# Another table of places for the steps of a four-layer transformer block: other order on every engine, other banks

## The chip, the cores and the metric

The kernel runs on one core of one Trainium2 chip. The metric is the device time in microseconds (us) of one execution. TensorE is written PE, VectorE DVE, ScalarE ACT, GpSimd POOL; PEld is the weight load of PE.

## What is computed

Eight samples of 512 rows by 256 columns pass four layers, each added to its input after a layer norm: causal attention with rotary embedding, gated attention over the 256 rows with the largest gate, attention with a relative bias, and gated attention again.

```python
x = x + attn_a(_layernorm(x), Wq, Wk, Wv, Wo)          # 16 heads of 16, rope, causal
x = x + ffn(_layernorm(x), Wg, Wq, Wk, Wv, Wo)         # top 256 of 512 rows by gate, 16 heads of 16
x = x + attn_b(_layernorm(x), w_qkv, w_out, rel_bias)  # 16 heads of 64, scores + bias
x = x + ffn(_layernorm(x), Wg, Wq, Wk, Wv, Wo)
```

Everything is in float32 but a few masks.

## The kernel before

The work is cut into 2264 steps, `Step(kind, s, l, n, q)`: kind, sample s, layer l, and indices n and q. A letter ahead of the kind names the layer: `c_` causal, `f_` gated (l is 1 or 3), `b_` biased. Most steps have a part on PE that fills one, two or four of the eight PSUM banks, and a part on DVE or ACT that empties them (`UNITS` says how many and by whom).

The steps that matter here:

- `b_k`, `b_q`, `b_v`: projections for a pair of heads (line 824), `b_row`: two score products of 64 rows (L1507), then on DVE bias and row maximum (L1229), then the exponential on ACT (L1038); `b_nrm`: reciprocal on DVE (L1238) and scaling on POOL (L961); `b_tr`: eight transposes (L1515), copied by ACT (L1047); `b_val`: the product with the values, in four parts q (L1525); `b_y`: output product (L1271).
- `c_xt`, `b_xt`: transposes of the normed input (L1290), copied by ACT (L980); `c_qk`: the first product that reads the copy of `c_xt` (L824). `c_p1`, `c_m`, `c_p2`, `c_val`: scores with 32 rows for the maxima (L1322, reduced by DVE, L1138), the maxima turned (L1335), scores again with the maxima in them (L1345, exponential on ACT, L998), values (L1359). `c_p1` and `c_p2` take four banks each.
- `f_row`, `f_rank`, `f_spread`, `f_gather`: the gate turned into a row, ranks, and the choice of 256 rows. `f_p1`, `f_m`, `f_p2`, `f_val`: as in the causal layer, for four groups n (L1432 with DVE L1209; L1441; L1450 with ACT L1016; L1462). `f_t1`: the results turned (L1470), divided on DVE (L1158); `f_ot`: turned back (L1478); then `f_o` and `f_y`.

PE runs in four shapes: the full 128 by 128, 32-row tiles (`c_p1`, `c_p2`, `f_p1`, `f_p2`), 64-row tiles (`b_row`), and 32 or 64 columns (`c_val` and `f_val`; `b_val`). The table `TILES` holds them. `c_p1` begins in 32-row tiles and ends in the full array.

What sets the order: `PLACE` gives every step a number. `turn` adds the sample's multiple of `CYCLE`. `in_order` takes, again and again, the step with the lowest number among those whose needs and forerunners are out; only the order comes from the numbers. It hands banks to the steps by its own table of costs (`WORK`). Every engine then walks this one list in order: PE, ACT, DVE, POOL and the queue of SP each issue their part of a step when the list comes to it. An engine that waits for one step holds back all its later ones. Line 842 is where PE's waits are issued (`at_least`).

Rows of the table: `first0`, `first1` and `first` for the causal and gated layers of samples 0 and 1 and the biased layer of sample 0; `cycle` for the causal and first gated layers of samples 2 to 7 and the biased layers of samples 1 to 6; `cycle3` for the last gated layers of samples 0 to 5; `last2`, `last` and `last1` for what ends the run. In the cycle of sample s, from `b_xt` of s to `b_xt` of s + 1, PE works on the biased layer of s, the last gated layer of s - 1, and the causal and first gated layers of s + 1. There are six such cycles with the same order, s = 1 to 6. Each has 240 PE steps.

Of the kernel before, what the change touches and what calls it, by code (L numbers as in the profile page):

```python
# [162 lines left out]
CYCLE = 2819  # L163
PLACE = {
    ("cycle", "b_k"): [940, 564, 782, 1543, 1850, 2107, 2827, 2871],
    ("cycle", "b_ln"): [398],
    ("cycle", "b_nrm"): [1019, 936, 764, 792, 1423, 1418, 1604, 1655, 1561, 1652, 896, 1550, 1761, 1614, 1568, 1732,
        1792, 2127, 2267, 1916, 2922, 2520, 2776, 2528, 3096, 2882, 3042, 3343, 2733, 2817, 3550, 2831],
    ("cycle", "b_q"): [663, 576, 766, 1637, 825, 2162, 2471, 2879],
    ("cycle", "b_row"): [975, 697, 248, 1003, 1032, 1492, 1319, 1182, 1616, 1223, 1375, 1474, 1731, 1516, 1675, 1739,  # L170
        1969, 1638, 2082, 2014, 2604, 2537, 2741, 2090, 2859, 2926, 3250, 2868, 3266, 3302, 2738, 3024],
    ("cycle", "b_tr"): [1099, 991, 1183, 1082, 1570, 1553, 1656, 1293, 1699, 1665, 1166, 1311, 1953, 1330, 1718,
        1585, 2348, 2655, 2060, 2702, 2958, 3018, 2788, 3112, 3129, 2929, 3344, 3453, 3286, 3445, 3584, 3407],
    ("cycle", "b_v"): [704, 978, 1361, 1307, 2154, 2840, 2851, 3414],
    ("cycle", "b_val"): [1309, 1312, 1221, 1229, 1751, 1061, 1504, 1531, 1630, 1169, 1237, 1400, 2100, 1769, 1824,
        2011, 2756, 2589, 2357, 2659, 3312, 2552, 3215, 3269, 3634, 3602, 3566, 3492, 3373, 3643, 3331, 3267],
    ("cycle", "b_xt"): [833],
    ("cycle", "b_y"): [3692, 3608, 3323, 3678],
    ("cycle", "c_ln"): [-1088],
    ("cycle", "c_m"): [-660, -470, -394, -292],  # L180
    ("cycle", "c_ot"): [-130, -106],
    ("cycle", "c_p1"): [-714, -726, -691, -679, -628, -526, -857, -496, -448, -1257, -361, -321],
    ("cycle", "c_p2"): [-724, -621, -1033, -1136, -1158, -445, -310, -893, -251, -619, -813, -585],
    ("cycle", "c_qk"): [-958, -951, -934, -869],
    ("cycle", "c_rot"): [-1197, -944, -1054, -1353, -919],
    ("cycle", "c_t1"): [-188, -132],
    ("cycle", "c_turn_k"): [-826, -741],
    ("cycle", "c_turn_q"): [-768, -674],
    ("cycle", "c_v"): [-838, -852],
    ("cycle", "c_val"): [-599, -517, -474, -421, -497, -342, -241, -425, -601, -169, -221, -450],  # L190
    ("cycle", "c_xt"): [-1065],
    ("cycle", "c_y"): [-75, -642],
    ("cycle", "f_gate"): [-389],
    ("cycle", "f_gather"): [90],
    ("cycle", "f_k"): [111],
    ("cycle", "f_ln"): [-45],
    ("cycle", "f_m"): [298, 231, 318, 406],
    ("cycle", "f_o"): [638],
# [12 lines left out]
    ("cycle3", "f_gather"): [3849],
    ("cycle3", "f_k"): [3860],
    ("cycle3", "f_ln"): [3234],
    ("cycle3", "f_m"): [4178, 4127, 4183, 4215],
    ("cycle3", "f_o"): [4465],
    ("cycle3", "f_ot"): [3649],
    ("cycle3", "f_p1"): [3989, 3954, 3950, 3911],
    ("cycle3", "f_p2"): [4087, 4027, 3843, 4190],
    ("cycle3", "f_q"): [3898],
    ("cycle3", "f_rank"): [3811],  # L220
    ("cycle3", "f_row"): [2966],
    ("cycle3", "f_spread"): [3829],
# [1379 lines left out]
```

How the kernel before makes its waits and increments, by code:

```python
            def at_least(engine, s, value):  # L838
                if value > reached.get((id(engine), s.num), 0):
                    reached[id(engine), s.num] = value
                    engine.wait_ge(s, value)
# [26 lines left out]
                @block.sync  # L869
# [9 lines left out]
                    for dst, src in ((wg, wg_f), (wqf, wq_f), (wkf, wk_f), (wvf, wv_f), (wof, wo_f), (wob, wo_b)):  # L879
                        sp.dma_start(dst[:], src).then_inc(w_rest, 16)
                    for i in range(2):
                        sp.dma_start(wb[:, i], w_b[i]).then_inc(wb_loaded[i], 16)
                        sp.dma_start(band[:, i], band_in[i]).then_inc(band_loaded[i], 16)
                    for now in plan.order:
                        kind, s, l, n, q = now
                        m = memory(now)
                        k = PAIRS * s + n
                        if kind == "b_row" and q == NT - 1 and k + 2 < pairs:
                            sp.wait_ge(dve_read, plan.unit(now, now, "o2"))
                            sp.dma_start(band[:, k % 2], band_in[(k + 2) % PAIRS]).then_inc(band_loaded[k % 2], 16)
                        if kind == "b_v" and k + 2 < pairs:
                            sp.wait_ge(act_full, plan.unit(now, now))
                            sp.dma_start(wb[:, k % 2], w_b[(k + 2) % PAIRS]).then_inc(wb_loaded[k % 2], 16)
                        if kind == "f_y" and l == 3:
                            sp.wait_ge(dve_read, plan.unit(now, now))
                            two = slice(2 * n, 2 * n + 2)
```

## Time and profile before

| what | value |
|---|---|
| median of 3 runs | 2244.47 us (2241.98 to 2245.79) |
| the profiled execution | 2247.84 us |
| its span | 2246.0 us |
| PE busy | 2152.3 us, 96% |
| PE weight loads busy | 1344.7 us, 60% |
| DVE, ACT, POOL busy | 60%, 52%, 24% |
| chain that ended last | PE 92%, ACT 4%, DVE 3% |

The page gives busy times by engine, the span in slices, and the chain of work that ended last. The timeline gives the start and the length of each group of instructions of one line. A matmul's record is longer than the distance to the next start, since they overlap; so a step's price on PE is read as the distance between starts.

### The profile page before, as it was taken

Reading aid. Unit: us, or ns where it says so; the run is one execution under the profiler, and the core shown is the slowest. Engines: PE = TensorE matmul, PEld = TensorE weight load, DVE = VectorE, ACT = ScalarE, POOL = GpSimd, SP = SyncE. Lnnn points to the kernel's source line nnn. Section 1 sums busy time; section 2 is a strip of 40 time slices with the busy share of each in tenths; the row PEclk is TensorE's granted clock in tenths of the full one; section 3 lists DMA queues with packets and bytes.
Section 4 is the critical chain, followed back from the end, with each engine's and each line's share of the span. In section 5 each row is a group of like instructions: output and inputs, shape, how many; then the busy total and the mean of one; then the engine's idle time right before and its main releaser. Section 6 shows DMA issues by size and latency. Waiting matters only on the chain.

```text
span 2246.0 us, 40133 instructions
## 1 busy us (share of the span) xinstructions
PE 2152.3 (96%) x15600; PEld 1344.7 (60%) x15616; DVE 1345.5 (60%) x3970; ACT 1163.5 (52%) x2625; POOL 530.7 (24%) x755
## 2 busy tenths in 40 slices
PE   7899999999999999999999999999999999999987
PEld 4456656655675556655666646665466655666655
DVE  7766554575555755657646567466664666746443
ACT  3453663645636555365554654456543656536632
POOL 3211231231212322132221421114211142112220
PEclk9999999999999999999999999999999999999997
DMA  3000121110112011020011200111001120111200
GB/s 127 2 2 31 64 71 55 66 41 32 41 31 83 24 32 41 32 83 25 32 41 39 76 25 31 41 55 59 25 32 48 48 76 9 47 38 64 73 1 10
DMA packets 29052, 98.25 MB, mean 44 GB/s; under 512 B 2881, under 2 KB 11457, under 8 KB 28737
## 3 DMA queue, kind: packets, MB, share of 16 engines
q1 hardware_dynamic: 28864, 95.70, 12.7%
q8 instruction: 125, 2.05, 0.4%
q14 instruction: 63, 0.51, 0.1%
HBM read 91.49 MB, written 4.19 MB: 43 GB/s over the span
## 4 chain that ended last, share of the span: by engine, by line
PE 92%; ACT 4%; DVE 3%; issue 1%; DMA 0%; POOL 0%; DVEq 0%
PE ps L824 26%; PE ps L1507 10%; PE ps L1271 10%; PE ps L1525 10%; PE ps L1515 10%; PE ps L1322 4%; PE ps L1345 3%; PE ps L1359 3%; PE ps L1450 3%; PE ps L1432 3%; PE ps L1462 3%; ACT PTc L998 2%; PE ps L1326 2%; ACT PTf L1016 1%; PE ps L1470 1%
## 5 line engine op out<-in xcount | busy, mean ns | idle before, releaser
L961 POOL TENSOR_SCALAR probs<-probs,rtotal 128x512 f32<-128x512 f32 x512 | 344.5, 694 | 931.1 <-DVE rtotal L1238 931.0
L1229 DVE CUSTOM_DVE_ANT_0 probs<-ps,band 128x512 f32<-128x512 f32 x512 | 332.9, 688 | 261.7 <-PE ps L1507 261.7
L1038 ACT ACTIVATE probs<-probs,peak 128x512 f32<-128x512 f32 x512 | 365.3, 714 | 212.6 <-DVE peak L1234 212.5
L1047 ACT ACTIVATE PT<-ps 128x512 f32<-128x512 f32 x512 | 263.5, 617 | 89.1 <-PE ps L1515 89.0
L1515 PE MATMUL ps<-ident,probs 128*128 128x128 f32 x2048 | 246.5, 274 | 0.8 <-POOL probs L961 0.4
L1507 PE MATMUL ps<-KT,QT 64*128 64x512 f32 x1024 | 246.0, 609 | 0.0
L1515 PEld LDWEIGHTS ps<-ident,probs 128*128 128x128 f32 x2048 | 226.8, 141 | 30.3 <-issue 21.4
L1138 DVE TENSOR_REDUCE mcol<-ps 128x1 f32<-128x384 f32 (+3 forms) x512 | 210.4, 481 | 55.9 <-PE ps L1326 55.8
L824 PE MATMUL ps<-xnT,wb 128*128 128x512 f32 x512 | 236.8, 602 | 1.7 <-ACT xnT L980 1.0
L1525 PE MATMUL ps<-PT,Vb 128*64 128x512 f32 x1024 | 230.3, 597 | 1.7 <-ACT PT L1047 0.9
L998 ACT ACTIVATE PTc<-ps 128x384 f32<-128x384 f32 (+1 forms) x384 | 168.2, 553 | 74.2 <-PE ps L1345 74.1
L1209 DVE TENSOR_REDUCE mcol<-ps 128x2 f32<-128x512 f32 x256 | 158.8, 684 | 42.7 <-PE ps L1432 42.5
L1016 ACT ACTIVATE PTf<-ps 128x512 f32<-128x512 f32 x256 | 132.8, 615 | 82.9 <-PE ps L1450 81.9
L824 PEld LDWEIGHTS ps<-xnT,wb 128*128 128x128 f32 x512 | 91.9, 190 | 117.1 <-issue 97.6
L1243 DVE TENSOR_TENSOR x<-x,ps 128x512 f32<-128x512 f32 x64 | 43.8, 685 | 193.2 <-PE ps L1271 193.2
L1525 PEld LDWEIGHTS ps<-PT,Vb 128*64 128x64 f32 x1024 | 69.4, 137 | 144.3 <-issue 137.9
L1507 PEld LDWEIGHTS ps<-KT,QT 64*128 64x128 f32 x1024 | 92.6, 186 | 93.5 <-issue 77.9
L953 POOL TENSOR_SCALAR_AFFINE_SELECT PTc<-PTc 128x512 f32<-128x512 f32 x128 | 80.7, 642 | 287.1 <-ACT PTc L998 287.1
L938 POOL TENSOR_TENSOR rstd<-veps,pow_half 128x2 f32<-128x2 f32 x64 | 47.0, 734 | 396.5 <-DVE veps L1068 396.5
L824 PEld LDWEIGHTS ps<-wb,xnT 128*128 128x128 f32 x1024 | 121.0, 192 | 20.2 <-issue 15.2
L824 PE MATMUL ps<-wb,xnT 128*128 128x128 f32 x1024 | 126.2, 277 | 0.0
L1345 PE MATMUL ps<-Qz,K 32*128 32x512 f32 (+3 forms) x1024 | 96.8, 469 | 25.4 <-ACT PTc L998 13.9
(127 smaller groups left out, 2963.8 us busy)
## 6 DMA issues: line engine op xcount, KB each, us to landing
band<-in_band SPq DMA_DIRECT2D x64, 896.0 KB, 4.5
wb<-in_w_b SPq DMA_DIRECT2D x64, 384.0 KB, 3.1
x<-in_x SPq DMA_DIRECT2D x16, 256.0 KB, 3.0
out<-x SPq DMA_DIRECT2D x16, 256.0 KB, 2.2
wob<-in_wo_b SPq DMA_DIRECT2D x1, 1024.0 KB, 7.8
wqk<-in_wqk_a SPq DMA_DIRECT2D x1, 512.0 KB, 5.4
wva<-in_wv_a SPq DMA_DIRECT2D x1, 256.0 KB, 4.9
woa<-in_wo_a SPq DMA_DIRECT2D x1, 256.0 KB, 5.2
```

What stands on the lines that cost most here:

```text
L824: last = nc.tensor.matmul(o, w, r, start=(i == 0), stop=(i == len(pairs) - 1))
L961: last = g.tensor_scalar(unit, unit, rtotal[:, r % 8, e:e + 1], 1.0, ALU.mult, ALU.mult)
L998: a.activation(pt_c(m, q)[:, h], bank(now, name)[:, 0:w], ACT.Exp).then_inc(act_read, 1)
L1038: last = a.activation(unit, unit, ACT.Exp, bias=peak[:, r % 8, e:e + 1], accum_out=total[:, r % 8, e:e + 1])
L1047: a.activation(PT[:, k % 2, e, :, tile_of(q)], bank(now, name).rearrange("p (k n) -> p k n", k=NT), ACT.Copy).then_inc(act_read, 1)
L1138: last = v.tensor_reduce(max_places(m.mcol[:, e, t, :], e)[:, h:h + 1], bank(now, name)[:, o:o + w], AXIS.X, ALU.max)
L1229: v.tensor_tensor_reduce(out=probs[:, r % ROWS_HELD, e, :], in0=bank(now, name), in1=band[:, k % 2, e, lo:lo + T], scale=1.0, scalar=-3e38 ...
L1271: last = te.matmul(o[:, j * D:(j + 1) * D], w, r, start=(k == 0 and j == 0), stop=(k == count - 1 and j == 1))
L1345: last = te.matmul(o[h][:, at_:at_ + w], m.K1[group(h), c, e, tile_of(t)], m.Qz[group(h), c, e, t * P:T], start=True, stop=True)
L1507: full(te.matmul(bank(now, name), QT2[half(e), k % 2, tile_of(q)], KT2[half(e), k % 2, :], start=True, stop=True), now, name)
L1515: last = te.transpose(bank(now, name)[:, tile_of(t)], probs[:, r % ROWS_HELD, e, tile_of(t)], ident[:])
L1525: last = te.matmul(o[half(e), :], Vb[:, k % 3, q, half(e)], PT[:, k % 2, e, q, :], start=(q == 0), stop=(q == NT - 1))
```

## The change

All 2264 steps stay, with the same operations, tiles and buffers. New are the constant `CYCLE` and every number of `PLACE`; with them the order on all engines changes, and the banks follow from it. The diff, cut to the rows spoken of:

```diff
-CYCLE = 2819
+CYCLE = 2805
 PLACE = {
...
-    ("cycle", "b_tr"): [1099, 991, 1183, 1082, 1570, 1553, 1656, 1293, 1699, 1665, 1166, 1311, 1953, 1330, 1718,
-        1585, 2348, 2655, 2060, 2702, 2958, 3018, 2788, 3112, 3129, 2929, 3344, 3453, 3286, 3445, 3584, 3407],
+    ("cycle", "b_tr"): [1264, 1531, 1558, 856, 1705, 754, 1776, 1844, 1974, 1350, 1374, 1973, 1434, 1770, 2296, 2323,
+        2715, 2578, 2997, 3032, 3150, 3152, 2302, 3222, 2481, 3321, 3248, 3370, 3445, 2374, 3206, 3859],
...
-    ("cycle", "b_row"): [975, 697, 248, 1003, 1032, 1492, 1319, 1182, 1616, 1223, 1375, 1474, 1731, 1516, 1675, 1739,
-        1969, 1638, 2082, 2014, 2604, 2537, 2741, 2090, 2859, 2926, 3250, 2868, 3266, 3302, 2738, 3024],
+    ("cycle", "b_row"): [1333, 1249, 638, 74, 1389, 1267, -298, -425, 1231, 1756, 1772, 1811, 709, 1202, 1267, 966,
+        2357, 1008, 2349, 1147, 2533, 1243, 2739, 1833, 2372, 2465, 2488, 2184, 1779, 2350, 3315, 3049],
...
-    ("cycle", "b_y"): [3692, 3608, 3323, 3678],
+    ("cycle", "b_y"): [3904, 3907, 3829, 4070],
...
-    ("cycle", "c_qk"): [-958, -951, -934, -869],
+    ("cycle", "c_qk"): [-1748, -1747, -958, -650],
-    ("cycle", "c_xt"): [-1065],
+    ("cycle", "c_xt"): [-617],
...
-    ("cycle", "f_t1"): [516, 603],
+    ("cycle", "f_t1"): [1037, 1062],
-    ("cycle", "f_ot"): [87],
+    ("cycle", "f_ot"): [1067],
...
-    ("cycle3", "f_t1"): [4327, 4407],
+    ("cycle3", "f_t1"): [4496, 4582],
-    ("cycle3", "f_ot"): [3649],
+    ("cycle3", "f_ot"): [4616],
...
```

Sorting the steps by the two tables gives the two orders. A stretch of PE's steps in the cycle of sample 3, before and after:

```
before  f_val.2 f_val.3 f_t1.0 b_k.3 b_tr.1.0 b_tr.1.1 f_t1.1 f_ot b_row.2.0 b_row.2.1 b_row.2.2 b_row.2.3 b_q.3 ...
after   f_val.2 f_val.3 b_row.2.2 b_tr.1.2 f_t1.1 b_row.2.3 b_row.3.0 f_ot b_tr.1.3 b_row.3.1 b_val.0.0 ...

before  ... b_val.2.2 b_val.2.3 c_xt b_k.4 b_q.4 c_qk.0 c_qk.1 c_qk.2 c_qk.3 b_tr.3.0 ...
after   ... b_tr.3.0 b_tr.3.1 b_v.3 c_xt c_qk.0 c_qk.1 c_qk.2 c_qk.3 b_k.4 b_q.4 b_tr.3.2 ...
```

(`b_row.2.3` is n = 2, q = 3; the `f_` steps are those of layer 3.)

## Rows read from the trace of the kernel before

**Rows 1.** The page: busy times (share of the span), and the chain by engine.

```profile
PE 2152.3 (96%) x15600; PEld 1344.7 (60%) x15616; DVE 1345.5 (60%) x3970; ACT 1163.5 (52%) x2625; POOL 530.7 (24%) x755
PE 92%; ACT 4%; DVE 3%; issue 1%; DMA 0%; POOL 0%; DVEq 0%
```

**Rows 2.** Windows: stretch, its length, busy us per engine (instructions), clock, DMA share, GB/s.

```profile
0.00:182.40 182.40, 155.09 (x1427) 91.01 (x1429) 129.95 (x332) 76.73 (x159) 43.87 (x67) 0.99 0.11 40
...
620.30:893.80 273.50, 266.94 (x1953) 166.89 (x1953) 167.22 (x496) 145.07 (x328) 65.76 (x92) 1.00 0.13 43
...
1987.90:2246.00 258.10, 233.71 (x1456) 153.32 (x1456) 121.10 (x365) 114.97 (x262) 46.07 (x68) 0.93 0.11 35
```

**Rows 3.** Timeline of PE: a `b_tr` ahead of a 32-row step, one ahead of a full-array step.

```profile
840.90 1.04 PE L1515 MATMUL ps<-ident,probs 128*128 128x128 f32 x8
841.87 1.15 PE L1432 MATMUL ps<-K1f,Qzf 32*128 32x256 f32 x16
...
872.19 1.04 PE L1515 MATMUL ps<-ident,probs 128*128 128x128 f32 x8
873.06 1.95 PE L824 MATMUL ps<-wb,xnT 128*128 128x128 f32 x16
```

**Rows 4.** Waits of PE, whole run: us in total, times, longest us.

```profile
PE ps L1478 <- DVE onf L1158: 17.0, 14, 1.6
...
PE ps L1387 <- DVE gate L1168: 5.7, 1, 5.7
PE ps L824 <- DVE above L1178: 5.1, 2, 3.9
```

**Rows 5.** Timeline of PE: the second `f_t1` and `f_ot`, in both gated layers of a cycle.

```profile
694.36 0.60 PE L1470 MATMUL ps<-ident,stripsf 128*128 128x128 f32 x4
696.09 0.65 PE L1478 MATMUL ps<-ident,onf 128*128 128x128 f32 x4 [1.13 <-DVE onf L1158]
...
874.85 0.60 PE L1470 MATMUL ps<-ident,stripsf 128*128 128x128 f32 x4
876.67 0.63 PE L1478 MATMUL ps<-ident,onf 128*128 128x128 f32 x4 [1.22 <-DVE onf L1158]
```

**Rows 6.** Timeline of PE: an `xt` ahead of a reader of its copy, and one with cover.

```profile
182.42 1.04 PE L1290 MATMUL ps<-ident,xn 128*128 128x128 f32 x8
184.41 1.12 PE L824 MATMUL ps<-xnT,wb 128*128 128x512 f32 x2 [0.96 <-ACT xnT L980]
...
725.09 1.09 PE L1290 MATMUL ps<-ident,xn 128*128 128x128 f32 x8
726.02 3.60 PE L824 MATMUL ps<-xnT,wb 128*128 128x512 f32 x8
```

**Rows 7.** Timeline of PE in the causal layer: `c_p2` right behind `c_p2`, and what follows.

```profile
778.33 1.14 PE L1345 MATMUL ps<-Qz,K 32*128 32x512 f32 x8
780.23 0.93 PE L1345 MATMUL ps<-Qz,K 32*128 32x384 f32 x8 [0.76 <-ACT PTc L998]
781.70 1.14 PE L1322 MATMUL ps<-K,Qz 32*128 32x512 f32 x8 [0.54 <-ACT PTc L998]
...
795.31 1.14 PE L1345 MATMUL ps<-Qz,K 32*128 32x512 f32 x8
796.38 0.85 PE L1359 MATMUL ps<-PTc,Vx 128*32 128x384 f32 x8
```

**Rows 8.** Timeline of PE in the first gated layer of a cycle.

```profile
851.06 0.38 PE L1441 MATMUL ps<-ident,mcol 128*128 128x128 f32 x2
851.96 1.15 PE L1432 MATMUL ps<-K1f,Qzf 32*128 32x256 f32 x16 [0.52 <-ACT PTf L1016]
```

**Rows 9.** The page, costliest groups: busy, mean ns of one, idle before.

```profile
L1515 PE MATMUL ps<-ident,probs 128*128 128x128 f32 x2048 | 246.5, 274 | 0.8 <-POOL probs L961 0.4
...
L1209 DVE TENSOR_REDUCE mcol<-ps 128x2 f32<-128x512 f32 x256 | 158.8, 684 | 42.7 <-PE ps L1432 42.5
L1016 ACT ACTIVATE PTf<-ps 128x512 f32<-128x512 f32 x256 | 132.8, 615 | 82.9 <-PE ps L1450 81.9
```

More of the change, by code:

```diff
@@ new lines @@
+    ("first0", "f_ot"): [2476],
+    ("first0", "f_p1"): [1771, 1710, 537, 1283],
+    ("first0", "f_p2"): [1595, 1741, 1663, 1769],
+    ("first0", "f_q"): [1684],
+    ("first0", "f_rank"): [1415],
+    ("first0", "f_row"): [1393],
+    ("first0", "f_spread"): [1321],
+    ("first0", "f_t1"): [2423, 2427],
+    ("first0", "f_v"): [1885],
+    ("first0", "f_val"): [2248, 1986, 2372, 1921],
+    ("first0", "f_y"): [2674, 366],
+    ("first1", "c_ln"): [-230],
+    ("first1", "c_m"): [1301, 1498, 1649, 1800],
@@ new lines @@
+    ("first1", "c_xt"): [544],
+    ("first1", "c_y"): [1720, 3178],
+    ("first1", "f_gate"): [1098],
+    ("first1", "f_gather"): [2296],
+    ("first1", "f_k"): [2341],
+    ("first1", "f_ln"): [1079],
+    ("first1", "f_m"): [2608, 2467, 3131, 3083],
+    ("first1", "f_o"): [3629],
+    ("first1", "f_ot"): [3381],
+    ("first1", "f_p1"): [2428, 2413, 2338, 1111],
+    ("first1", "f_p2"): [2414, 1780, 2954, 2489],
+    ("first1", "f_q"): [2301],
+    ("first1", "f_rank"): [2021],
+    ("first1", "f_row"): [1815],
@@ new lines @@
+    ("last1", "f_k"): [26885],
+    ("last1", "f_ln"): [29288],
+    ("last1", "f_m"): [29446, 29362, 32785, 30465],
+    ("last1", "f_o"): [29734],
+    ("last1", "f_ot"): [30753],
+    ("last1", "f_p1"): [29354, 29271, 27905, 29342],
+    ("last1", "f_p2"): [29194, 30013, 28474, 29254],
+    ("last1", "f_q"): [27571],
+    ("last1", "f_rank"): [26897],
+    ("last1", "f_row"): [29231],
+    ("last1", "f_spread"): [26291],
+    ("last1", "f_t1"): [31728, 31980],
+    ("last1", "f_v"): [28357],
@@ new lines @@
+    ("last1", "f_val"): [32839, 30195, 32425, 29836],
+    ("last1", "f_y"): [29426, 31015],
+    ("last2", "f_gate"): [20149],
+    ("last2", "f_gather"): [22202],
+    ("last2", "f_k"): [22530],
+    ("last2", "f_ln"): [20713],
+    ("last2", "f_m"): [23761, 23920, 24818, 24301],
+    ("last2", "f_o"): [26565],
+    ("last2", "f_ot"): [26129],
+    ("last2", "f_p1"): [23370, 23187, 24338, 21746],
+    ("last2", "f_p2"): [24136, 22331, 24864, 23657],
+    ("last2", "f_q"): [22586],
+    ("last2", "f_rank"): [22086],
@@ L355 @@
+    ("last2", "f_row"): [21411],
+    ("last2", "f_spread"): [20278],
+    ("last2", "f_t1"): [24840, 25907],
+    ("last2", "f_v"): [23543],
+    ("last2", "f_val"): [24782, 22803, 25547, 24134],
+    ("last2", "f_y"): [26759, 24913],
 }
```

297 lines of the change are left out of this document (119 added, 178 removed).

## The prediction

> **What bounds the kernel now.** I read the page first [rows 1]: PE is busy for 96% of the span and holds 92% of the chain, DVE and ACT have 40% and 48% of their time free. So the time is that of PE's list of steps: the work of the steps, what lies between them, and the waits. The windows come next, cut at the starts of `b_xt` [rows 2]. The six cycles are alike, 273.5 us each, 266.94 us of them busy; the run is a head up to 182.4 us, the biased layer of sample 0 (164.3 us), six cycles, and an end of 258.1 us. A price in the cycle counts six times; that is where to look.
>
> PE's busy time can't be taken as work, for a record is longer than the distance to the next start. So I took the distances between the starts. For every kind of step the least distance is nearly constant: a `b_tr` is 0.87 us where the next step keeps the shape of the array (872.19 to 873.06) and 0.97 where it changes it (840.90 to 841.87) [rows 3]. The least distances of the 240 steps of one cycle (its group is the window from 620.3 us [rows 2]), summed, are 251.2 us. The shape changes 93 times, which at 0.094 us is 8.7. Waits of over 0.15 us, read the same way, are 8.3, and small delays at steps that wait for a semaphore (34 of about 0.1 us), with rests, are 5.3. That makes 273.5. The 251.2 stay; the change plays with the other 22.
>
> The Trainium skill, in "Perfetto Trace Analysis", Identifying the Most-Contended Engine, says that matmul busy time is no measure of how near PE is to its limit and wants the busy share of the weight loads. Here that is 60% against 96% [rows 1]; by the first figure one would expect more room than there is, and the sum here goes by starts.
>
> **The change part by part.** The order behind each count is the table, sorted under the needs of the steps.
>
> *Changes of shape.* The new order alternates finely: in a cycle a `b_tr` stands right ahead of a `b_row` 14 times in place of once, and a `b_row` ahead of a `b_tr` 5 times in place of never. The shape changes 117 times in a cycle in place of 93, 881 times in all in place of 726. 155 x 0.094 = +14.6 us. From the rows it is 0.10 at the one place [rows 3], and the same within 0.01 us at `b_val`, `b_row`, `f_m` and `c_turn_k`. Bounds: a change in front of a wait is hidden by it, so if a third is hidden, +10; none hidden, +15.
>
> On this the Trainium skill has a rule against the change: "TensorEngine Tiling (Array Packing)", Key Properties, says that switching the tiling mode drains TensorE. It gives no time. The trace agrees that a switch costs, by 0.094 us each [rows 3].
>
> *The wait at `f_ot`.* Before, the second `f_t1` stands right ahead of `f_ot`, in both gated layers of a cycle, and DVE's reciprocals and products lie open between them. From start to start it is 1.73 and 1.82 us, where four transposes alone take 0.44 [rows 5]: 1.29 + 1.38 = 2.7 us a cycle. (The view of waits says 17.0 us at 14 places [rows 4], a little less, as the record's end covers some.) After, two steps stand between, of two `b_row` or two `b_val`, 1.7 us and more: the wait goes, 6 x 2.7 = -16.0. In the first gated layer of sample 0 two `c_val` of 1.5 us come between: -1.4. In the last layer of all nothing can. Together -17.4. What is late next there is the copy by ACT between `f_ot` and `f_o`, and it has one step of 0.86 us over it, just enough. If DVE comes late to `f_t1` since `b_row` stands ahead in its queue, up to half of the gain is lost: -9 to -17.4.
>
> *`c_xt` ahead of `c_qk`.* Before, `b_k` and `b_q` cover ACT's two copies of `c_xt` (725.09 to 726.02, no wait). After, `c_qk` stands right behind `c_xt` in all six cycles. The same thing happens once before, at `b_xt` of sample 0: 182.42 to 184.41, 1.99 us in place of 0.93 [rows 6]. +1.06 x 6 = +6.4. Bounds: ACT is behind by a `b_v` copy, +10; it is never less than the copies themselves, +6.
>
> *Banks in the causal layer.* `c_p2` takes four banks and ACT needs longer to empty them than PE to fill them. A `c_p2` of the same size with a `c_val` behind it takes 1.07 us, 0.09 of them the change of shape (795.31 to 796.38); with another `c_p2` right behind it, 1.90 in place of 0.98 (778.33 to 780.23), and the `c_p1` behind that costs another 0.7 (780.23 to 781.70) [rows 7]. Before, a cycle has three such pairs (0.92, 0.92, 1.03), the 0.70, and 0.36 and 0.23 at `c_m` and `c_val`: 4.2 us of the 8.3. After, it has three pairs again (the two behind the first `c_p2` of group 0, and one in group 1); the others have other steps between them. I take the pairs as they are and let most of the 1.3 go: -6 us in all. Bounds: all of it goes, -25; or the eight banks are held as often by `b_row` and `b_tr` in between, +6.
>
> *The gated layers.* Before, there are 1.5 us of other waits per cycle: 0.59 behind an `f_m` (851.06 to 851.96 in place of 0.31) [rows 8], and three smaller ones. A group n needs four reductions of 684 ns on DVE and four exponentials of 615 ns on ACT [rows 9], some 2.5 us of each, overlapped. After, the second `f_p2` follows the first with one `f_m` or `b_val` between while `f_p1` of the next group still holds four banks; that leaves about 0.6 us open in one layer and 0.5 us in the other; `f_rank` has 3.5 us over DVE's 3.7 in the first gated layer, which leaves 0.3 to 0.4; `f_t1` has two steps over ACT's queue, perhaps 0.4. I take 2.3 us in place of 1.5: +5 in all. Bounds: all covered, -9; twice as much, +14.
>
> *Small delays.* They come where two semaphores are waited for. More steps follow one of another reader's banks now. +1, from -3 to +6.
>
> *Head and end.* In the head PE is not busy for 27.3 us [rows 2], and the chains in it stay the same: layer norm of sample 0, rotation, the way from `c_y` to `f_row` where PE has 3.9 us of steps in both. A pair of `c_p2` less: -1. At the end the last gated layer runs alone. In the new order `f_m` of the other group comes behind three `f_p1`, so the first `f_p2` starts one group of reductions (2.5 us) later, but the second then follows at once: 0, from -2 to +3. The mean clock of the end was 0.93 [rows 2], and the waits for the gate and the ranks, 5.7 and 3.9 us [rows 4], have nothing over them in either order.
>
> *DMAs.* The refill of `x` follows the last `f_y` of a sample; PE has 12.6 us of steps from there to `c_xt` in place of 13.9. Before, the load landed ahead of its reader and DVE did not wait. 0; if it did, it would be DVE alone.
>
> Sum: 14.6 - 17.4 + 6.4 - 6 + 5 + 1 - 1 = +2.6 us. The profiled execution was 2247.84 us, 3.4 above the median of 2244.47, so I make it 2250.4 on that scale and 2247.1 as a median.
>
> **The rivals.** *Even feeding.* `b_row` and `b_tr` in turn give DVE and ACT their work evenly, so banks come free in time. Then the three pairs cost half as much (-1.4 us a cycle) and a quarter of the gated waits goes (-0.6): 12 us less than my sum, 2235. For it speaks that DVE and ACT are idle for 40% and more [rows 1]; against it that three pairs stand unchanged.
>
> *Queues in order.* Slower than before: DVE and ACT also walk the one list. In the gated layers `b_row`, with two long passes on each of them, now stands between `f_p2`, `f_val` and `f_t1`, so their readers come late, and PE stops for a bank or a copy. At 2.5 us a cycle more than taken it is +15: 2262. The point from which a cycle is longer than before is 5.9 us of waits in it (273.5 less 251.2, less 11.0 for 117 changes, less 5.4 of small delays), where it has 8.3 now. For it: my own terms, 2.8 + 1.1 + 2.3, already make 6.2. Against: the groups of four reductions and exponentials are priced in them as they ran [rows 9].
>
> *A full drain at each change.* A transpose's record is 274 ns [rows 9] at a distance of 109 (0.87 by eight [rows 3]). If the switch from `b_tr` to `b_row` waited for the whole record, it would cost 0.165, and the 155 more would be 25.6 in place of 14.6: 2258. The row says 0.10 ahead of a 32-row step [rows 3], so little is left for it. The Trainium skill's page "TensorEngine Tiling (Array Packing)" calls it a drain, with no time.
>
> **How the numbers follow.** Forecast (a sum between 0 and +5): 0.35, split over no change and slower at its edge. Even feeding 0.32, queues 0.29, full drain 0.04. About 0.2% of the time, 4.5 us, is what a measurement can tell from no change. Faster 0.34 (even feeding, and a little of the forecast's lower side), same 0.31, slower 0.35. As signs are so even, the forecast's own range is 2242 to 2252; the range for 8 in 10 takes in most of both others, 2230 to 2264.
>
> **What would show it.** In the profile after: cycles of 273.5 to 274.5 us between the `b_xt`; `f_ot` gone from the waits but for the last layer (some 2 us in place of 17.0); a wait of `c_qk` for ACT's copy at six places, near 1 us each; `b_tr` still 0.97 ahead of `b_row`; three waits of about 0.9 at `c_p2` in a cycle. The prediction is wrong if the cycle is under 272 (even feeding) or over 275.5 (queues, seen as waits at L1450, L1462 and L1470, or drain, seen as `b_tr` above 1.0).

## The result and the profile after

The kernel after takes 2252.33 us (median of 7 runs, 2250.85 to 2255.65), the kernel before beside it 2244.47 (7 runs, 2241.98 to 2248.79): 1.0035 of the time before, 95% interval 1.0023 to 1.0046. The forecast was 2247.1, with 2230 to 2264 as the range. So the change is slower by some 8 us, inside the range, and 5 us above the forecast. The profiled execution is one of 2252.26 us.

The page after, in answer to [rows 1]; the busy times, and the chain by engine:

```profile
PE 2176.6 (97%) x15600; PEld 1334.3 (59%) x15616; DVE 1365.0 (61%) x3970; ACT 1166.9 (52%) x2625; POOL 527.4 (23%) x755
PE 91%; DVE 5%; ACT 3%; issue 1%; POOL 0%; DVEq 0%
```

PE has the same 15600 matmuls, and 24.3 us more of busy time: 2176.6 in place of 2152.3. No operation was added, so the same instructions hold PE longer. That is the first thing to see; spread over the 155 more changes of shape it would be 0.157 us each.

The windows, cut at the starts of `b_xt` as in [rows 2] (stretch, length, PE busy, PEld busy, DVE, ACT, POOL, clock, DMA share, GB/s):

```profile
0.00:179.50 179.50, 154.84 (x1427) 90.86 (x1429) 131.76 (x332) 76.65 (x159) 43.29 (x67) 1.00 0.11 41
179.50:342.50 163.00, 161.97 (x1021) 98.92 (x1020) 91.37 (x298) 101.58 (x236) 46.14 (x68) 1.00 0.19 65
342.50:628.50 286.00, 281.60 (x2001) 174.69 (x2002) 172.72 (x503) 145.97 (x328) 66.00 (x93) 1.00 0.13 42
628.50:904.00 275.50, 271.23 (x1952) 165.51 (x1953) 170.18 (x496) 145.81 (x328) 65.32 (x92) 1.00 0.13 43
904.00:1179.60 275.60, 271.13 (x1952) 165.44 (x1953) 170.07 (x496) 145.70 (x328) 65.31 (x92) 1.00 0.13 43
...
2006.30:2250.50 244.20, 222.00 (x1407) 142.38 (x1407) 118.34 (x358) 113.72 (x262) 45.40 (x67) 0.94 0.11 37
```

A cycle is 275.6 us in place of 273.5. (The first one holds three more `b_y` of 3.45 us, which the end no longer has: 286.0 less 10.4 is 275.6.) Segment by segment: six cycles +12.4, biased layer of sample 0 -1.4, head -2.9, end -3.5 (258.1 before, 244.2 + 10.4 after). That is +4.6, and the spans differ by 4.5. (The profiled execution of before was 3.4 above its median, which is most of what is missing to 8.) The loss is in the cycles.

The waits of PE, whole run (us in total, times, longest), in answer to [rows 4]:

```profile
...
PE ps L824 <- ACT xnTc L980: 7.4, 8, 1.0
PE ps L1345 <- DVE mcol L1138: 6.7, 7, 1.4
PE ps L1345 <- ACT PTc L998: 6.0, 11, 1.2
PE ps L1387 <- DVE gate L1168: 5.7, 1, 5.7
PE ps L824 <- DVE pick L1188: 4.6, 6, 0.8
...
PE ps L1478 <- DVE onf L1158: 1.6, 1, 1.6
```

The wait of `f_ot` went from 17.0 us at 14 places to 1.6 at one. The copy of `c_xt` is waited for at 8 places. The gather's wait for `pick` is new. By the distances between starts, waits of over 0.15 us in a cycle fell from 8.3 to 6.6 us. So the waits did what they were meant to, by 1.7 us a cycle, and the cycle is still 2.1 longer.

### The profile page after: what moved, and what is told of

It is laid out like the page before. It is cut to its first block, busy times and chain, and to the rows that moved or that the text cites. A ratio compares the mean times of both kernels' runs of the same rounds, so it can differ in the third digit from the quotient of the medians.

```text
span 2250.5 us, 40154 instructions
## 1 busy us (share of the span) xinstructions
PE 2176.6 (97%) x15600; PEld 1334.3 (59%) x15616; DVE 1365.0 (61%) x3970; ACT 1166.9 (52%) x2625; POOL 527.4 (23%) x755
## 4 chain that ended last, share of the span: by engine, by line
PE 91%; DVE 5%; ACT 3%; issue 1%; POOL 0%; DVEq 0%
PE ps L824 25%; PE ps L1507 10%; PE ps L1271 10%; PE ps L1515 10%; PE ps L1525 9%; PE ps L1322 4%; PE ps L1345 4%; PE ps L1359 3%; PE ps L1450 3%; PE ps L1432 3%; PE ps L1462 3%; PE ps L1326 2%; ACT PTc L998 1%; PE ps L1441 1%; DVE probs L1229 1%
## 5 line engine op out<-in xcount | busy, mean ns | idle before, releaser
L1047 ACT ACTIVATE PT<-ps 128x512 f32<-128x512 f32 x512 | 268.9, 607 | 77.9 <-PE ps L1515 77.9
L1507 PE MATMUL ps<-KT,QT 64*128 64x512 f32 x1024 | 260.6, 620 | 0.0
L1515 PE MATMUL ps<-ident,probs 128*128 128x128 f32 x2048 | 257.4, 275 | 0.0
L1138 DVE TENSOR_REDUCE mcol<-ps 128x1 f32<-128x128 f32 (+3 forms) x512 | 210.3, 482 | 55.8 <-PE ps L1326 55.8
L1525 PE MATMUL ps<-PT,Vb 128*64 128x512 f32 x1024 | 242.4, 602 | 0.0
L1525 PEld LDWEIGHTS ps<-PT,Vb 128*64 128x64 f32 x1024 | 64.3, 136 | 125.2 <-issue 109.7
L1507 PEld LDWEIGHTS ps<-KT,QT 64*128 64x128 f32 x1024 | 86.7, 185 | 87.5 <-issue 63.9
L1271 PE MATMUL ps<-wob,OTb 128*128 128x256 f32 x512 | 113.9, 379 | 0.8 <-DVE OTb L1240 0.8
```

Source lines behind the costliest of these rows:

```text
L1047: a.activation(PT[:, k % 2, e, :, tile_of(q)], bank(now, name).rearrange("p (k n) -> p k n", k=NT), ACT.Copy).then_inc(act_read, 1)
L1138: last = v.tensor_reduce(max_places(m.mcol[:, e, t, :], e)[:, h:h + 1], bank(now, name)[:, o:o + w], AXIS.X, ALU.max)
L1271: last = te.matmul(o[:, j * D:(j + 1) * D], w, r, start=(k == 0 and j == 0), stop=(k == count - 1 and j == 1))
L1507: full(te.matmul(bank(now, name), QT2[half(e), k % 2, tile_of(q)], KT2[half(e), k % 2, :], start=True, stop=True), now, name)
L1515: last = te.transpose(bank(now, name)[:, tile_of(t)], probs[:, r % ROWS_HELD, e, tile_of(t)], ident[:])
L1525: last = te.matmul(o[half(e), :], Vb[:, k % 3, q, half(e)], PT[:, k % 2, e, q, :], start=(q == 0), stop=(q == NT - 1))
```

## Where the time went: the price of a change of shape

I put every PE step of the two cycles side by side. The 251.2 us of least distances are the same. The exits from a shape are 11.0 us (117 x 0.094) in place of 8.7. What I had called small delays is 6.8 us in place of 5.3, and 6.1 of the 6.8 (before, 4.5 of the 5.3) lie in the step right behind a change. The least distances from start to start, alike to 0.002 us in both kernels where both have the case:

| step | same shape on both sides | changed behind it | changed ahead of it | both |
|---|---|---|---|---|
| `b_row` | 0.858 | 0.955 | 0.962 | 1.059 |
| `b_tr` | 0.873 | 0.966 | 0.928 | 1.023 |
| `b_val` | 0.858 | 0.958 | 0.909 | 1.009 |
| `b_q` | 1.716 | 1.812 | 1.820 | 1.914 |

So a change costs twice: 0.094 at the end of the old shape, which the prediction had, and for these steps 0.05 to 0.10 at the start of the new one, which it had not. The trace of before holds it. These are the matmuls of L1507 in the first `b_row` of a group of four, and in the next (duration in ns, min/median/max):

```profile
L1507 PE MATMUL ps<-KT,QT x4: 589/641/693, 988.0 to 988.5; 64*128 64x512 f32 x4
...
L1507 PE MATMUL ps<-KT,QT x6: 589/589/589, 988.5 to 989.4; 64*128 64x512 f32 x6
```

Behind a change two of the four records are 693 ns, 104 more than 589; in the steady shape none is. In a `b_tr` behind a change one record of eight is 328 ns in place of 272.

The weight loads of the same `b_row` show where the delay comes from (the matmuls of a `b_row` start two at a time, and so do their loads):

```profile
987.96 0.30 PEld L1507 LDWEIGHTS ps<-KT,QT 64*128 64x128 f32 x4 [0.17 <-issue]
988.49 0.19 PEld L1507 LDWEIGHTS ps<-KT,QT 64*128 64x128 f32 x2 [0.23 <-issue]
```

The first two loads start with the first two matmuls, at 987.96, and the next two 0.107 us behind them; the second pair of matmuls is late by 0.104. In the steady shape each pair of loads starts with a pair of matmuls, 0.43 us apart. It is the same at all 150 `b_row` behind a change in after (past 200 us), and with 0.053 at `b_val` and about 0.055 at `b_tr`. The kind of operation is not the cause: in the full array a `b_tr` right behind a projection has no delay (0.109 us from the first to the second transpose; 0.165 behind a change). But the delay does not belong to changes of shape alone. The first `c_qk`, which in after waits 1 us for the copy of `c_xt` with the same shape on both sides, has it at all six places; its first product ends up 105 ns longer:

```profile
L824 PE MATMUL ps<-wqk,xnTc x4: 592/592/697, 1000.2 to 1001.6; 128*128 128x512 f32 x4
```

A change and a wait together do not cost it twice (`f_p2` behind both is late by 0.10 at most).

## Experiments

All are kernels with the same steps, operations and tiles; only places in the order differ. `behind(order, x, y)` takes x out of the order and puts it behind y, and is called ahead of `in_order`. Line numbers in them are 37 to 61 higher. Each was timed beside the kernel before; ratios are to that. A cycle is the distance from `b_xt` to `b_xt`; within one trace it repeats within 0.3 us unless two figures are given. (In after and the kernels made from it the first cycle is counted without its three `b_y`.)

| kernel | us, median | ratio, 95% interval | cycle |
|---|---|---|---|
| before | 2244 to 2246 | 1 | 273.5 |
| after | 2252.33 | 1.0035, 1.0023 to 1.0046 | 275.6 |
| tr_row_turns | 2250.15 | 1.0023, 1.0010 to 1.0036 | 274.6 |
| more_changes | 2275.73 | 1.0142, 1.0122 to 1.0162 | 277.6 or 279.2 |
| fewer_turns | 2260.91 | 1.0069, 1.0049 to 1.0089 | 276.5, one of 278.3 |
| grouped | 2565.6 | 1.1431, 1.1411 to 1.1451 | 324.2 |
| xt_covered | 2262.73 | 1.0086, 1.0069 to 1.0103 | 276.7 |
| ot_covered | 2239.18 | 0.9976, 0.9966 to 0.9985 | 272.1 |
| values_between | 2249.72 | 1.0020, 1.0009 to 1.0032 | 274.2 |
| vb_tr | 2261.13 | 1.0068, 1.0050 to 1.0086 | 276.1 or 277.6 |
| vb_fv | 2256.31 | 1.0049, 1.0031 to 1.0068 | 275.3, one of 275.8 |
| head_after | 2245.88 | 1.0001, 0.9991 to 1.0012 | 273.5 |
| head_and_ot | 2242.36 | 0.9980, 0.9966 to 0.9993 | 273.0, one of 272.6 |
| both_gains | 2237.58 | 0.9968, 0.9956 to 0.9980 | 272.1, one of 272.6 |

### The price of a change, alone: tr_row_turns

The theory: a change costs 0.17 us where `b_tr` and `b_row` alternate, and waits have no part in it. The rivals: 0.094, or nothing because even feeding pays it back.

```diff
 # kernel before
+    for s in range(1, B - 1):
+        for q in range(4):
+            behind(order, Step("b_row", s, 2, 3, q), Step("b_tr", s, 2, 2, q))
```

> The kernel before, with one thing changed in the six cycles: the four b_tr of n = 2 and the four b_row of n = 3, which stand behind each other as two groups, alternate. That is 6 more changes of shape per cycle (36 in all) between exactly the two shapes that the change under study alternates, and no cover is taken from anything. The prediction's price of 0.094 us, all of it at the end of the old shape: +0.56 us per cycle, +3.4 in all. The theory after the result, a change also delays the second matmul of the new shape (0.105 us into b_row, 0.057 into b_tr), so 0.17 on average: +1.0 to +1.1 us per cycle, +6.4 in all. Even feeding (DVE and ACT get their work in turns, so waits shrink): 0 or less.

The timeline of PE in the stretch, kernel before (start, length, engine, line; four `b_tr` in one row, then four `b_row`, then `b_val`):

```profile
984.37 3.66 PE L1515 MATMUL ps<-ident,probs 128*128 128x128 f32 x32
987.96 3.70 PE L1507 MATMUL ps<-KT,QT 64*128 64x512 f32 x16
991.59 1.08 PE L1525 MATMUL ps<-PT,Vb 128*64 128x512 f32 x4
```

The same eight steps in tr_row_turns:

```profile
986.85 1.04 PE L1552 MATMUL ps<-ident,probs 128*128 128x128 f32 x8
987.81 1.13 PE L1544 MATMUL ps<-KT,QT 64*128 64x512 f32 x4
988.87 1.09 PE L1552 MATMUL ps<-ident,probs 128*128 128x128 f32 x8
989.89 1.13 PE L1544 MATMUL ps<-KT,QT 64*128 64x512 f32 x4
...
994.06 1.13 PE L1544 MATMUL ps<-KT,QT 64*128 64x512 f32 x4
995.12 1.51 PE L1562 MATMUL ps<-PT,Vb 128*64 128x512 f32 x6
```

From the first `b_tr` to `b_val` it was 7.22 us (984.37 to 991.59) and is 8.27 (986.85 to 995.12). A `b_tr` has 1.02 (988.87 to 989.89) and a `b_row` 1.06 (987.81 to 988.87), as in the table. The cycle is 274.57 in place of 273.53: +1.04 for six changes, 0.174 each. The waits over 0.15 us are the same twelve places and 8.3 us. This shows the fuller price and excludes both rivals here.

### More and fewer changes with their side effects: more_changes, fewer_turns, grouped

```diff
 # kernel before: more_changes
+    for s in range(1, B - 1):
+        for q in range(4):
+            behind(order, Step("b_row", s, 2, 3, q), Step("b_tr", s, 2, 2, q))
+        behind(order, Step("b_k", s, 2, 6), Step("b_val", s, 2, 4, 0))
+        behind(order, Step("b_q", s, 2, 6), Step("b_val", s, 2, 4, 1))
```

> The order of before with 10 more changes of shape in each cycle and nothing else: four b_tr and four b_row in turn, and b_k, b_q of pair 6 put between the parts of a b_val; 786 changes in place of 726. Theory (a change costs 0.094 us at its end and 0.05 to 0.105 behind the first matmul of the new shape): 0.15 to 0.2 each, +9 to +12 us. Rival one (the 0.094 of the prediction is all): +5.6. Rival two (even feeding of DVE and ACT pays for the changes): 0 or less.

Measured 30 us slower, far over all three. The ten changes cost 1.7 us a cycle (0.17 each). The rest was mine: `b_k` and `b_q` of pair 6 had stood over DVE's gate. In the waits, `f_row` for the gate (L1387 in [rows 4], L1426 here) goes from 5.7 us once to

```profile
PE ps L1426 <- DVE gate L1207: 18.5, 7, 5.7
```

that is 2.40 us of distance per cycle, and in three of the cycles 1.54 more at the `b_row` of pair 6. The run agrees with the price only after these are taken off.

```diff
 # kernel after: fewer_turns
+    for s in range(1, B - 1):
+        behind(order, Step("b_row", s, 2, 3, 2), Step("b_tr", s, 2, 2, 1))
+        behind(order, Step("b_tr", s, 2, 5, 0), Step("b_tr", s, 2, 4, 3))
+        behind(order, Step("b_row", s, 2, 6, 2), Step("b_tr", s, 2, 5, 1))
+        behind(order, Step("b_row", s, 2, 7, 0), Step("b_tr", s, 2, 5, 3))
```

> The kernel after, with four neighbouring swaps of b_tr and b_row in each of the six cycles that join steps of one shape: 111 changes of shape per cycle in place of 117, the rest of the order as it is. By the prediction's price of 0.094 us: 0.56 us less per cycle, 3.4 in all. By the fuller price (0.17 us for b_tr and b_row, its end and the delay behind the first matmul): 1.0 us less per cycle, 275.6 to 274.6, 6 us in all, some 2246 us. If the alternation is what keeps banks free, as even feeding says, new waits of 0.2 us and more appear at the joined steps and the cycle is no shorter.

A miss in the total: the cycle grew to 276.5. With `b_tr` 5.0 and `b_row` 6.2 gone from their places, nothing stands between `c_t1` and `c_ot`, and the timeline shows it (`c_t1`, `c_ot`):

```profile
1100.36 1.09 PE L1407 MATMUL ps<-ident,strips 128*128 128x128 f32 x8
1103.38 0.66 PE L1415 MATMUL ps<-ident,on 128*128 128x128 f32 x4 [1.93 <-DVE on L1197]
```

This wait is 2.14 us of distance, where after has 0.17. Less the difference, the cycle is 274.5, 1.1 below that of after, where 6 x 0.174 is 1.0. The other joined places have no new wait. (One of the six cycles is 1.7 us longer still, by more waits.)

In grouped, the kernel after has a look-ahead: where the next PE step would change the shape, a `b_` step of the present shape is taken forward from among the next six. In short:

```diff
 # kernel after: grouped
+        if pick.kind in UNITS and shape(pick) != at:
...
+                if x.kind in UNITS and shape(x) == at and x.kind[2:] in ("tr", "row", "val", "k", "q", "v") \
+                        and x.kind[0] == "b" and not ahead[x] & set(left[:i]):
+                    pick = x
```

> The order of after, but a b_ step of the shape that the array has is taken ahead of one that would change it, from up to six steps on: 657 changes in place of 881. Theory (0.15 us per change): -34 us against after, less what waits for banks come back, about -25, so faster than before by some 15. Rival one (0.094 each): -21 less the waits, about -12. Rival two (the fine turns of b_tr and b_row keep the banks coming, and grouping them brings the waits back): no gain or slower than after.

The second rival, and far past it: where 25 us less than after was expected, it is over 300 us slower. It has 83 changes in a cycle in place of 117 and takes 324 us for it. The changes did cost less (7.8 us of exits and under 4 of small delays), but the waits rose from 6.6 to 61 us a cycle, above all where a step was taken ahead of its own input:

```profile
PE ps L1576 <- POOL probs L1022: 55.1, 16, 4.6
PE ps L1531 <- ACT stripsf L1080: 37.3, 16, 5.2
PE ps L885 <- DVE pick L1249: 18.4, 12, 3.1
```

Few changes are no aim by themselves: 34 of them are worth 5 to 6 us a cycle, and the covers that were given up for them 55.

### The waits one by one: xt_covered, ot_covered

```diff
 # kernel after: xt_covered
+    for s in range(1, B - 1):
+        behind(order, Step("b_k", s, 2, 4), Step("c_xt", s + 1, 0))
+        behind(order, Step("b_q", s, 2, 4), Step("b_k", s, 2, 4))
```

> The order of after with b_k and b_q of pair 4 back between c_xt and c_qk in all six cycles, same number of changes (881). Theory: the wait for the two copies, 1.06 us, goes: -6.4 us against after. Rival (the rotation behind c_qk comes 3.4 us later and c_turn waits for it): -3 us or less.

The rival, and more than it: the wait of 1.06 us at `c_qk` is gone, and 2.31 us came in its place, further on, where the rotated rows of POOL are turned:

```profile
1020.49 1.53 PE L1348 MATMUL ps<-ident,qk 128*128 128x128 f32 x12 [2.15 <-POOL qk L983]
```

The two projections of 3.4 us had been the cover between `c_qk` and `c_turn_q`; now they stand ahead of `c_qk`. So the change's new wait can't be mended by this swap: at these places there is one cover for two waits, and after leaves the smaller one open.

```diff
 # kernel before: ot_covered
+    for s in range(B - 1):
+        if s < 6:
+            behind(order, Step("b_q", s + 1, 2, 3), Step("f_t1", s, 3, 1))
+            behind(order, Step("f_ot", s, 3), Step("b_q", s + 1, 2, 3))
+        if s > 0:
+            behind(order, Step("f_ot", s + 1, 1), Step("b_tr", s, 2, 7, 0))
+    behind(order, Step("f_ot", 0, 1), Step("c_val", 1, 0, 3, 1))
```

> The order of before with one part of the change alone: a step or two between the second f_t1 and f_ot, at 13 places (six of the last gated layer, six of the first, one in the head); no more changes of shape in the cycles (93 each, 2 more in the head). Theory (waits and shapes add up on PE): the 1.30 and 1.39 us per cycle go, b_v or b_tr copies on ACT give 0.2 back: -13 to -16 us, cycles of about 271. Rival (waits move on, since DVE and ACT set the pace behind PE): the time comes back as waits at f_o or at the next banks, -5 us or less.

Faster, with half of what was expected: 6.5 us, and 1.4 of the 2.7 us a cycle. From `f_t1` to `f_ot` no wait is left (692.90, 693.34, 695.05), but two steps on PE now come before POOL has scaled their input, and wait:

```profile
692.90 0.60 PE L1511 MATMUL ps<-ident,stripsf 128*128 128x128 f32 x4
693.34 1.88 PE L865 MATMUL ps<-xnT,wb 128*128 128x512 f32 x4
695.05 0.60 PE L1519 MATMUL ps<-ident,onf 128*128 128x128 f32 x4
...
702.84 1.04 PE L1556 MATMUL ps<-ident,probs 128*128 128x128 f32 x8
704.36 1.09 PE L1556 MATMUL ps<-ident,probs 128*128 128x128 f32 x8 [0.49 <-POOL probs L1002]
```

0.66 us there, 0.18 at another `b_tr`, and 0.5 more of small delays. A wait that goes pulls everything behind it forward, and what had been just in time is late.

### Are the bank waits open time? values_between, vb_tr, vb_fv

```diff
 # kernel before, with ot_covered: values_between (first four lines), vb_tr and vb_fv (one more each)
+            behind(order, Step("b_nrm", s + 1, 2, 1, 3), Step("b_row", s + 1, 2, 2, 0))
+            behind(order, Step("c_val", s + 1, 0, 0, 0), Step("c_p2", s + 1, 0, 0, 1))
+            behind(order, Step("c_val", s + 1, 0, 0, 2), Step("c_p2", s + 1, 0, 1, 0))
+            behind(order, Step("c_val", s + 1, 0, 1, 2), Step("c_p2", s + 1, 0, 2, 0))
+            behind(order, Step("b_tr", s, 2, 6, 0), Step("f_m", s + 1, 1, 0))
+            behind(order, Step("f_v", s + 1, 1), Step("f_spread", s + 1, 1))
```

> ot_covered with two more moves in the six cycles. The DVE and POOL part of b_nrm n = 1, q = 3 is moved ahead, behind b_row n = 2, q = 0 (it came 0.66 us late for its b_tr). And a c_val is put between the two c_p2 of each of the three pairs: its PE work is there anyway, and takes the place of the wait for a bank. 94 changes of shape in place of 93. If the bank waits were open time, as the prediction's term for banks in the causal layer had it, each pair's 0.92, 0.92 and 1.03 us shrinks to some 0.1: -2.5 us per cycle, and -0.6 for the b_tr, +0.2 for the change: 272.1 to some 269.3, 17 us in all. If ACT with its exponentials is what paces the causal layer, the same time comes back at the next c_p2 or c_p1, as a wait for PTc, and the cycle stays above 271.

The second outcome. All three pairs of `c_p2` are free of waits (1042.75 to 1043.61 to 1044.71), and the causal layer waits at seven other places:

```profile
1042.75 0.93 PE L1390 MATMUL ps<-Qz,K 32*128 32x384 f32 x8
1043.61 1.06 PE L1404 MATMUL ps<-PTc,Vx 128*32 128x512 f32 x8
1044.71 0.94 PE L1390 MATMUL ps<-Qz,K 32*128 32x256 f32 x16
1046.27 1.14 PE L1367 MATMUL ps<-K,Qz 32*128 32x512 f32 x8 [0.62 <-ACT PTc L1043]
...
1051.63 0.94 PE L1367 MATMUL ps<-K,Qz 32*128 32x128 f32 x16 [0.61 <-DVE mcol L1183]
...
1053.76 1.14 PE L1390 MATMUL ps<-Qz,K 32*128 32x512 f32 x8 [0.64 <-DVE mcol L1183]
...
1057.59 1.14 PE L1367 MATMUL ps<-K,Qz 32*128 32x512 f32 x8 [1.03 <-ACT strips L1045]
```

The waits of the layer sum up to some 6 us where they were 4.2. A `c_val` needs a bank of its own, which ACT empties; that this is why it was no free cover is likely, but no run parts it from the new order of ACT's work. The early `b_nrm` took away the 0.66 at `b_tr`, and 0.81 came back one step later, at `f_y`, for ACT's copy of `f_o`.

> values_between with b_tr of n = 6, q = 0 moved ahead between f_m and f_p1 of the first gated layer in a cycle, where the kernel before waits 0.59 us for a bank that ACT holds, and 0.43 behind that f_p1. No change of shape more or less. If the wait is open time: up to -1.0 us per cycle. If DVE's four reductions behind that f_p1 are then late for f_m of n = 2, 0.5 to 1 us comes back there and the cycle is as in values_between.

Slower by another 1.9 us a cycle, and by my own placing: `b_tr` 6.0 came ahead of POOL's scaling and waits 2.01 us for it. A further 0.80 came at an `f_m`, for DVE's maxima, as the second outcome had it, and the 0.59 and 0.43 us are gone. Since the 2.01 us alone would give the banks time to come free, it says nothing of the bank.

> values_between with f_v of the first gated layer in a cycle moved from between two f_p1 to behind f_spread: 92 changes of shape in place of 94 per cycle. By the fuller price -0.3 us per cycle, by the prediction's -0.19. But f_v covers the bank wait between the two f_p1 (each takes four banks and DVE needs 2.7 us to empty them); if that matters, 0.5 to 1.1 us comes back at the second f_p1, as it does in the head, where two of them stand together.

Two changes fewer, -0.3 us in exits and small delays, and +1.4 in waits: with `f_v` gone from between the two `f_p1`, three new waits of 0.3 to 0.6 us stand behind them. 275.3 in place of 274.2.

### The head, and what is left as a gain: head_after, head_and_ot, both_gains

`HEAD` holds the first 343 steps in the order of after; the two kernels have the same set of steps there.

```diff
 # kernel before
+    steps = [x for x, _, _ in whole()]
+    order[:len(HEAD)] = [steps[i] for i in HEAD]
```

> The kernel before with the first 343 steps (the head and the biased layer of sample 0, up to b_xt of sample 1) in the order of the kernel after, and everything from there on in its own. Tells whether the gain of the head stands by itself: the traces say 182.4 to 179.5 us and 164.3 to 163.0 us, together -4.3. If it does, the span is 4.3 us shorter than before, cycles at 273.5 us, and so the six cycles and the end alone hold the whole loss of the change. The prediction's own figure for the head was -1.

No difference that can be measured. The biased layer of sample 0 takes 163.0 us as in after, 1.4 less. But the head is 182.4 us long, not 179.5. The windows of this stretch, in after, in both_gains and in head_after, all with one order, say why (the clock is the third number from the end):

```profile
100.00:120.00 20.00, 14.20 (x165) 7.77 (x165) 19.55 (x58) 7.21 (x16) 3.20 (x5) 1.00 0.00 1
```
```profile
100.00:120.00 20.00, 15.54 (x156) 7.84 (x156) 17.57 (x53) 6.73 (x16) 3.18 (x5) 0.83 0.00 1
```
```profile
100.00:120.00 20.00, 15.40 (x146) 7.69 (x145) 16.71 (x54) 7.29 (x16) 3.71 (x5) 0.74 0.01 2
```

At 1.00 the head is 179.5 us, at 0.83 it is 180.5, at 0.74 it is 182.4. Six traces with the head of after give 179.5 to 183.1, the seven others 182.4 to 183.6 (three with the head of before, four with `f_ot` covered in it). At the same clock in this stretch the head of after is the shorter one by some 2 us at 0.83 (180.5 to 181.0 against 182.5 and 183.0) and by some 0.5 at 0.74 (182.4 and 183.1 against 183.0 and 183.6). So of the 2.9 us that two single profiles show, one or more may be the execution's; the 1.4 are the order's, as they came back in every trace.

head_and_ot is head_after with ot_covered, and with `b_tr` 1.3 put behind the second `f_y`:

> head_after, with f_ot covered as in ot_covered, and b_tr of n = 1, q = 3 moved behind the second f_y, since its input from POOL came 0.66 us late there. If the terms add up: -4.3 from the head, -9 from f_ot as measured, and up to -4 from the wait at that b_tr: a span of 2229 to 2233 us, cycles of 271.5 us. If ACT or the copy of f_o is then late for f_y, the wait returns there and the cycle stays at 272.1.

A miss: the span is 2242.2 us, and the cycle 273.0, longer than the 272.1 of ot_covered. The wait returned, larger, 1.66 us at `f_y` for the copy of `f_o` (L1332 waits for ACT 8.1 us at 6 places): that `b_tr` had been its cover. both_gains leaves it where it was:

> The kernel before with the first 343 steps (the head and the biased layer of sample 0) in the order of the kernel after and f_ot covered in the cycles as in ot_covered; nothing else is moved. The two pieces of the change that the runs so far show as gains by themselves, without its extra changes of shape. Cycles of 272.1 us as in ot_covered, the biased layer of sample 0 in 163.0 in place of 164.3, the head 180 to 183. If they add up: 2238 us, 0.3 to 0.4% faster than before and some 14 us faster than after. If they do not, the head is no gain, as head_after already hints, and it is the 2239 of ot_covered or a little more.

2237.58 us, 0.32% faster than before (0.20 to 0.44%) and some 15 us faster than after. It has the lowest time here, but its lead over ot_covered, timed apart at 0.9976, is within the two intervals.

## Why the prediction was near, and what in it was wrong

Per step of the sum, predicted and measured (six cycles, by the distances between starts):

| term | predicted | measured |
|---|---|---|
| changes of shape, exits | +14.6 in all | +13.5 in the cycles |
| small delays | +1 | +9 |
| `f_ot` | -17.4 in all | -16.1 in the cycles |
| `c_xt` ahead of `c_qk` | +6.4 | +6.4 |
| banks in the causal layer | -6 | -10.6 |
| waits of the gated layers | +5 | +10 |
| head and biased layer of sample 0 | -1 | -1.4, and the clock's share |
| end | 0 | -3.5 in one pair of traces, most of it the clock's (below) |

The step that failed is the price of a change of shape. The count was right, 117, and so was 0.094 for the exit. The +1 for "small delays at steps that wait for a semaphore" was mis-sized and had the wrong cause: nine tenths of them stand at the entry into a new shape, and they grow with the changes. One change is 0.15 us on average ((8.7 + 5.3) / 93 before, (11.0 + 6.8) / 117 after), the 155 more some 24 us and not 14.6 + 1. With 24 the sum is +11 in place of +2.6, and the forecast a clear "slower". I had found the least distance of each kind of step, and a least distance is by its nature one with the same shape on both sides; I then asked what the next step costs it, never what the step ahead does.

The rival "a full drain at each change" had nearly the right sum, 25.6, and was given 0.04. Its sign came true as well, a `b_tr` above 1.0 us ahead of `b_row`, and would have been read for it. Its mechanism is still not what the runs show: it put 0.165 at the end of `b_tr`, and that end costs 0.094 as before; the rest is at the start of the same `b_tr`. [rows 3] spoke against the rival rightly and for my price wrongly, since it shows one side of the change only. The rule that the prediction took from the Trainium skill, "TensorEngine Tiling (Array Packing)", Key Properties, that switching the mode drains the array, agrees with 0.094 at the exit. It does not say that the entry has a price too.

The waits went as forecast in sum: -10.6 us predicted for the cycles (-16.0 + 6.4 - 6 + 5), some -10 measured. Not in their parts. Of the three pairs of `c_p2` that "stand unchanged", one waits 1.03 and the others 0.59 and 0.18. The first waits for banks that DVE's maxima hold, not for ACT; why the others are shorter no run here parts out:

```profile
1043.93 1.14 PE L1345 MATMUL ps<-Qz,K 32*128 32x512 f32 x8
1045.94 0.93 PE L1345 MATMUL ps<-Qz,K 32*128 32x384 f32 x8 [0.87 <-DVE mcol L1138]
1047.30 0.94 PE L1345 MATMUL ps<-Qz,K 32*128 32x256 f32 x16 [0.43 <-ACT PTc L998]
```

And the gated layers give twice the rise that I had, most at a place that I had not named, the gather behind a single `b_tr`:

```profile
1123.04 1.09 PE L1515 MATMUL ps<-ident,probs 128*128 128x128 f32 x8
1124.90 1.35 PE L824 MATMUL ps<-pick,xn 128*128 128x256 f32 x5 [0.76 <-DVE pick L1188]
```

"Queues in order" expected that, at 2.5 us a cycle more than forecast; it is 0.9 more. "Even feeding" had a piece of the truth at the `c_p2` pairs, 4.6 us in all beyond the forecast, which the gated layers gave back; tried alone, in tr_row_turns, it moved no wait. Of what should show each step, `f_ot` (1.6 us left) and `c_qk` came true; the cycle at 275.6 is just past the bound of 275.5 that was set for being wrong, and `b_tr` between two `b_row` is 1.02, past the 0.97.

That the median is within 5 us is in part luck. The six cycles were to be 3.9 us longer in all (13.5 - 16.0 + 6.4 - 6 + 5 + 1) and are 12.4; the head, the biased layer of sample 0 and the end were to be 1.4 shorter and are 7.8 in the two traces, in part by the clock. These errors have opposite signs, and nothing in the prediction ties them.

How much of the end is the order's stays open. From the last `b_xt` to the start of the last step on PE, ten traces with the end of before take 246.0 to 253.2 us, mean 251.0, and three with the end of after 245.4 to 248.5, mean 246.9 (the three `b_y` added). Most of that is the clock. The end in tr_row_turns (order of before) and in fewer_turns (order of after), at nearly one clock:

```profile
1994.60:2245.90 251.30, 227.62 (x1458) 149.17 (x1456) 120.94 (x365) 114.83 (x262) 46.02 (x68) 0.97 0.11 36
2015.20:2255.60 240.40, 218.03 (x1409) 139.45 (x1407) 118.09 (x358) 113.73 (x262) 45.41 (x67) 0.96 0.11 38
```

With 10.4 us for the three `b_y` the second is 250.8 us against 251.3. Two more such pairs, after with vb_tr and xt_covered with values_between, differ by 1.1 and 1.4 us. So some 0.5 to 1.5 us may be the order's; no run changed the end alone.

## What to carry to other kernels

Price a change of PE's array shape from both sides: the distance of the step ahead of it and that of the step behind it, each against the same step with the same shape around it and no wait ahead. Here they were 0.09 and 0.05 to 0.10 us, so alternating two kinds of short steps of 0.86 us costs about a fifth of each. When PE's busy time rises with the same number of instructions, look for records that grew before looking for waits.

A cover is worth what stands behind it. Seven of the twelve kernels here moved steps to save a wait or a change of shape and lost more where the steps had been. Ask of each moved step what it covered in its old place, and expect a part of a removed wait to come back: in ot_covered, the cleanest case here, it was half.

## What the runs showed of the hardware

Entering a shape delays the second matmul (in row tiles, the second group of matmuls), not the first: in the 64-row tiles and in full-array products by 0.10 us, for transposes and 64-column products by 0.05. The second matmul is late by as much as its weight load is: 0.107 us behind the first matmul at `b_row`, where in the steady shape the load starts with the matmul ahead of its own. The loads themselves have not grown (L1507: median 187 ns before, 186 after). The same 0.10 us stands behind a wait of PE with no change of shape (`c_qk`, six places). So in these traces it is the price of a start without a weight load ahead, whether a change or a wait led to it. Why a change keeps the load from running ahead, no run here tells.

The granted clock of the head, from 100 to 120 us, was 1.00 in the profiled execution of after and 0.83 or 0.74 in five others of the same order. These are means of full clock (2.4 GHz) and some 7 or 10 us at the lower level (1.2 GHz), behind waits of 1.45 and 1.90 us with little work between. The same product of four transposes behind the wait of 1.90 us is 0.62 us in after, at full clock, and 1.09 in head_after:

```profile
106.15 0.62 PE L1387 MATMUL ps<-ident,gate 128*128 128x128 f32 x4 [1.90 <-ACT PTc L998]
```
```profile
106.28 1.09 PE L1442 MATMUL ps<-ident,gate 128*128 128x128 f32 x4 [1.90 <-ACT PTc L1053]
```

Differences of up to 3.6 us in the head (179.5 to 183.1) and 7 in the end (246.0 to 253.2), each within one order, are therefore no property of the order. In a comparison of some 8 us the cycles, at clock 1.00 and alike within 0.2 us in the traces of before and after, told more than the span.
